# Filing stage of a graph layer: the low half of the normed x made by TensorE instead of VectorE

## The reference, cut to what matters

```python
def _layernorm(x, axis=-1, eps=1e-05):
    m = jnp.mean(x, axis=axis, keepdims=True)
    v = jnp.var(x, axis=axis, keepdims=True)
    return (x - m) / jnp.sqrt(v + eps)

edge_index_t = jnp.stack([src, dst], axis=1)
xn = _layernorm(x, axis=-1)          # x: (6250, 256), f32
x = x + gnn(xn, edge_index_t, ...) + mix(xn[None], ...)[0]
x = x + ffn(_layernorm(x, axis=-1)[None], ...)[0]
```

## Time and profile before

| | |
|---|---|
| time, median of 3 runs | 2389.4 us (2388.9 to 2390.93) |
| span of the profiled execution | 2388.4 us |
| TensorE busy (matmul) | 2128.0 us, 89% |
| VectorE busy | 1612.0 us, 67% |
| ScalarE busy | 1203.0 us, 50% |
| GpSimd busy | 358.6 us, 15% |

### The profile page before, as it was taken

How to read it: one execution, slowest core, us unless ns; L and a number is a source line. 1 busy time by engine, 2 the same in 40 slices (tenths; PEclk the granted TensorE clock), 3 DMA queues, 4 the chain that set the end, 5 groups by cost and what they waited for, 6 DMA issues and landing times.

```text
span 2388.4 us, 53411 instructions
## 1 busy us (share of the span) xinstructions
PE 2128.0 (89%) x15340; PEld 1319.0 (55%) x15341; DVE 1612.0 (67%) x4907; ACT 1203.0 (50%) x2432; POOL 358.6 (15%) x435
## 2 busy tenths in 40 slices
PE   3555557999999999999799999999999998799997
PEld 2444445555555555555355554444444443699996
DVE  6999998799999999999434342454454455455554
ACT  3445455455555555555555553444444444466664
POOL 1000000000000000000101010112112112366665
PEclk9765666899999999999899999999999999799998
DMA  3111112522222222222212114555555554555552
GB/s 81 40 34 34 39 32 71 180 111 117 111 117 110 111 120 110 119 110 117 96 51 101 51 69 177 186 207 189 189 207 188 190 206 164 166 97 91 90 92 46
DMA packets 131006, 275.62 MB, mean 115 GB/s; under 512 B 30478, under 2 KB 83903, under 8 KB 128755
## 3 DMA queue, kind: packets, MB, share of 16 engines
q1 hardware_dynamic: 103411, 221.23, 26.3%
q0 software_dynamic: 25856, 47.15, 8.8%
q10 hardware_dynamic: 1664, 6.35, 0.7%
HBM read 137.14 MB, written 132.95 MB: 113 GB/s over the span
## 4 chain that ended last, share of the span: by engine, by line
PE 80%; DVE 8%; DVEq 4%; issue 4%; DMA 1%; POOL 1%; ACT 1%; ACTq 0%; SPq 0%; POOLq 0%
PE bank L2131 45%; PE bank L2122 6%; PE bank L2352 6%; PE bank L2337 6%; PE bank L2284 5%; PE bank L2272 5%; DVE big L1043 2%; PE bank L2287 2%; DVE big L1057 1%; PE bank L2319 1%; DVEq L1072 1%; DVEq L1040 1%; DVEq L1053 1%; PE bank L2139 1%; PE bank L2000 1%
## 5 line engine op out<-in xcount | busy, mean ns | idle before, releaser
L2131 PE MATMUL bank<-RW,big 128*128 128x512 f16 (+1 forms) x4900 | 1180.9, 380 | 4.8 <-DMA big<-a_dram 4.6
L2131 PEld LDWEIGHTS bank<-RW,big 128*128 128x128 f16 x4900 | 443.9, 98 | 401.6 <-issue 9.1
L1793 ACT ACTIVATE big<-bank 128x512 f16<-128x512 f32 (+1 forms) x640 | 371.7, 581 | 318.8 <-PE bank L2122 318.8
L1190 DVE TENSOR_TENSOR big<-iotaB,keys 128x512 f16<-128x512 f16 x1300 | 452.3, 419 | 7.9 <-issue 7.8
L2122 PEld LDWEIGHTS bank<-big 128*128 128x128 f16 x2560 | 191.0, 98 | 111.7 <-issue 1.3
L2122 PE MATMUL bank<-big 128*128 128x128 f16 x2560 | 247.5, 219 | 0.4 <-issue 0.4
L908 POOL DMA_INDIRECT out_dram<-big x112 | 178.6, 1594 | 119.5 <-ACT big L1950 85.8
L844 POOL DMA_DIRECT2D big<-in_L_ffn_W_dram x8 | 6.4, 802 | 1144.1 <-DVE R L1249 1141.8
L1941 ACT ACTIVATE big<-bank,b1A,iscA 128x256 f32<-128x256 f32 x224 | 114.3, 560 | 101.1 <-PE bank L2337 97.6
L2352 PE MATMUL bank<-RW,big 128*128 (+1 forms) x1344 | 158.1, 275 | 0.0
L2337 PE MATMUL bank<-big,RW 128*128 128x256 f16 x1344 | 157.0, 274 | 0.2 <-ACT big L1930 0.2
(11 more groups left out here) (397 smaller groups left out, 2975.9 us busy)
## 6 DMA issues: line engine op xcount, KB each, us to landing
big<-a_dram SPq DMA_DIRECT2D x49, 832.0 KB, 5.9
big<-a_dram SPq DMA_DIRECT2D x49, 768.0 KB, 4.2
a_dram<-big SPq DMA_DIRECT2D x49, 640.0 KB, 3.0
a_dram<-big SPq DMA_DIRECT2D x49, 512.0 KB, 2.6
a_dram<-big SPq DMA_DIRECT2D x49, 448.0 KB, 2.5
big<-rows_dram SPq DMA_DIRECT2D x56, 265.0 KB
big<-in_x_dram SPq DMA_DIRECT2D x96, 128.0 KB, 2.1
big<-in_L_ffn_W_dram POOLq DMA_DIRECT2D x16, 512.0 KB, 4.6
```

The costliest lines, as they stand in the source:

```text
L1190: last = v.tensor_tensor(out[q].rearrange("p b (m k) -> p b m k", k=2), inturn(iotaB[:, :], QB, P // 2), twice(kd[:, q * QB:(q + 1) * QB, ...
L1793: a.activation(Ab[q][:, 0:n], banks[BB(q)][:, 0:n], ACT.Copy).then_inc(s_ab, 1)
L2131: last = mm(bank[:, :], blk(q, c), src, start=(u == 0), stop=(u == T))
```

## The change

VectorE's `low` goes, with the tile xlo and the semaphore s_xl. Instead `gram(t)` gets a group of two products in the right half of bank 5: xs with identS (f32, S on its diagonal) and then the high half in R2 with minus16 (f16, minus one on its diagonal), which together are S xs minus the high half. ScalarE evicts the low half from there. s_xt is signalled by the last of these products rather than by the last Gram product. GpSimd writes the two constants, ahead of its second signal. SyncE's blanking of R3 waits for the last s_xt.

```diff
@@ GpSimd, constants
             nc.gpsimd.memset(ident16[:, :], 0.0)
+            nc.gpsimd.memset(identS[:, :], 0.0)
+            nc.gpsimd.memset(minus16[:, :], 0.0)
...
-            for m in (ident, ident16):
-                nc.gpsimd.affine_select(out=m[:, :], in_=m[:, :], compare_op=ALU.not_equal, fill=1.0,
+            for m, one in ((ident, 1.0), (ident16, 1.0), (identS, S), (minus16, -1.0)):
+                nc.gpsimd.affine_select(out=m[:, :], in_=m[:, :], compare_op=ALU.not_equal, fill=one,
                                         base=0, pattern=[[-1, P]], channel_multiplier=1)
@@ SyncE, after the loop
-            sp.wait_ge(s_xl, T)
+            sp.wait_ge(s_xt, 1 + T)
             blank(0, at_pairs // D)
@@ VectorE
-            def low(t):
-                dve.wait_ge(s_xhi, t + 1)
-                dve.wait_ge(s_xlo, t + 1)
-                v.scalar_tensor_tensor(out=xlo, in0=xs[:, 0:D], scalar=S, in1=R2[:, bass.ds(t * 2 * D, D)],
-                                       op0=ALU.mult, op1=ALU.subtract).then_inc(s_xl, 1)
...
                 ranks(t, t % 2)
-                low(t)
@@ ScalarE
             def normal1(t):
                 act.wait_ge(s_stat, t + 1)
                 act.wait_ge(s_xt, t + 1)
-                if t:
-                    act.wait_ge(s_xl, t)
...
                 place1(t)
-                act.wait_ge(s_xl, t + 1)
-                a.activation(R2[:, bass.ds(t * 2 * D + D, D)], xlo, ACT.Copy, scale=S).then_inc(s_xlo, 1)
+                a.activation(R2[:, bass.ds(t * 2 * D + D, D)], banks[5][:, D:2 * D], ACT.Copy, scale=S).then_inc(s_xlo, 1)
@@ TensorE, gram
                 pe.wait_ge(s_xtc, t + 1)
+                pe.wait_ge(s_xlo, t + 1)
                 for h in range(2):
                     nc.tensor.transpose(banks[5][:, h * P:(h + 1) * P], xs[:, h * P:(h + 1) * P], ident[:, :])
                 for h in range(2):
-                    last = mm(banks[6 + h][:, 0:D + 1], xs[:, h * P:(h + 1) * P], xs[:, 0:D + 1],
-                              start=False, stop=False)
-                last.then_inc(s_xt, 1)
+                    mm(banks[6 + h][:, 0:D + 1], xs[:, h * P:(h + 1) * P], xs[:, 0:D + 1],
+                       start=False, stop=False)
+                mm(banks[5][:, D:2 * D], identS[:, :], xs[:, 0:D], start=True, stop=False)
+                pe.wait_ge(s_xhi, t + 1)
+                mm(banks[5][:, D:2 * D], minus16[:, :], R2[:, t * 2 * D:t * 2 * D + D], start=False, stop=True)\
+                  .then_inc(s_xt, 1)
@@ TensorE, after the loop, before bank 5 is used again
             pe.wait_ge(s_xtc, T + 1)
+            pe.wait_ge(s_xlo, T + 1)
```

More of the change, by code:

```diff
@@ L160, in gps_layer @@
         ident = sb("ident", [P, P])
+        identS = sb("identS", [P, P])
+        minus16 = sb("minus16", [P, P], F16)
         zeros16 = sb("zeros16", [P, P], F16)
@@ L264, in gps_layer @@
         xs = sp1.f32(D + 1)
-        xlo = sp1.f32(D)
         Gs = sp1.f32(2 * (D + 1)).rearrange("p (k n) -> p k n", k=2)
@@ L420, in gps_layer @@
         s_xhi = sem("s_xhi")
-        s_xl = sem("s_xl")
         s_xlo = sem("s_xlo")
```

## The result

The changed kernel takes 2373.02 us, the median of 4 runs (2371.35 to 2375.86), against 2389.39 before (4 runs as well), 16.4 us less. The two medians stand as 0.9931; the ratio estimated from all their runs is 0.9926, with an interval of 0.9912 to 0.994. Two later measurements gave 2374.66 (2373.01 to 2375.19) and 2373.76 us (2372.47 to 2373.95) for the same kernel. Each against the kernel before that ran beside it, the gain is 15.3 to 16.4 us, while VectorE's term alone, all of it kept, is 15.9.

The account below looks back on a forecast made before the run. VectorE was taken to bound the filing stage, with TensorE mostly at its slow clock. Terms -15.9 + 0.8 + 2.8 + 1.8 + 0.6 = -9.9 us took the span from 2388.4 to 2378.5, so median 2379.5; range 2375 to 2394.

Parts of the forecast that it names:

- VectorE's term: Filing stage: without `low`, 48 tiles each save 0.33 us of VectorE, 15.9 us in all.
- The constants' sum: Opening: GpSimd's two memsets and two selects delay its last select and the start by 0.8 us, all exposed.
- The tail: End of the filing stage: ScalarE waits for the last x tile, so the last two tiles can't shorten: 0.6 us.
- Charged beyond 5.88: Filing stage: losses above VectorE's new period, from restarts 2.8, falls in mid-group 1.8 and the tail 0.6 us.
- the start and six restarts: Start and after each `prepare`: TensorE begins slow, next reciprocal 0 to 0.8 us late; 7 x 0.4 = 2.8 us.
- the falls in mid-group: Filing stage: the clock falls about once in each of seven groups, mostly absorbed by slack; 7 x 0.25 = 1.8 us.
- Restless clock: Filing stage: clock falls again after some 6.6 us, 23 rounds at some 0.5 us: 2386.4 us; chance 0.23.
- TensorE becomes the bound: Filing stage: slow share stays 70%, 34 of 49 tiles take 7.2 us, 44 us lost: 2418 us; chance 0.12.
- Nearly all is kept: Filing stage: clock falls only in `prepare`, each restart hidden: -13.1 us, 2376 us; chance 0.13.
- Waiting for the deviation in place of `low`: Filing stage: VectorE waits for ScalarE instead, slow period some 6.05 us, half of 0.33 kept there; no separate chance.
- What would show it: Trace signs of being right: period 5.88, stage clock 0.8 or more, opening 0.8 us longer, fast `file1` just behind R1.
- the signs against it: Idle before reciprocals, `file1` right behind new products, `gram` over 3.6 us slow or 2.0 fast, mean clock under 0.7.

Follow-up runs that it names:

- four products more: Changed kernel with four more overwritten f32 products with identS per tile, ahead of the two that count: 2394.26 us, ratio 1.0018.
- the first experiment: Changed kernel without the two new products per tile, a copy of the transposed tile evicted as low half: 2378.18 us, ratio 0.9951.

## Why the prediction came out short

**VectorE's term was right.** The period goes from 6.21 to 5.88 us, to the hundredth.

**The constants' sum was right, and partly by luck.** 0.8 was charged as 0.3 for the memsets and 0.5 for the selects. In the nine profiles with the constants in front the first reciprocal is 0.6 to 1.0 us late, and it is back at 38.3 when they are made later. But the memsets cost nothing, and an idle of 0.4 us that nobody had foreseen stands in their place.

**The tail was about right.** It was charged for the last x tile, so it belongs to the last of the 48 periods. That one is 6.53, 7.32 and 6.27 us long in the three profiles, where 6.39 less the 0.33 would be 6.06: 0.5, 1.3 and 0.2 us lost, against 0.6. The way from the last reciprocal to the last `file1`, 0.4, 0.1 and 1.0 us longer, stood in no term.

**The failed step is "Charged beyond 5.88": the start and six restarts at 2.8 us and the falls in mid-group at 1.8.** Against the old 366.36 us less 48 x 0.33, the periods of the changed kernel lost 1.7, 2.4 and 0.3 us in its three profiles, a mean of 1.5, tail included, where these two terms and the tail had charged 5.2. Where the losses stand can be read from the waits for ScalarE's deviation: behind the start and the restarts 0.66, 0.62 and 0 us, against 2.8; behind falls in mid-group 0.19, 0.15 and 0, against 1.8. (In the last tile they are 0.25, 1.04 and 0. What is left, 0.3 to 0.6 us in each profile, is a balance of small idles of VectorE for which the profile names no wait and of tiles that had waited before.) The number of falls was about right: one in each of seven groups was expected, and the first profile has eight. What they cost was not. There are three reasons:
- The new products were priced by the ends of rows. 1.17 us slow and 0.67 fast were charged, and 1.07 and 0.54 measured (the fast f16 product is 269.47 to 269.58 in the timeline of four products more): a row's duration holds about 0.2 us in which the next instruction already runs (1.06 against 0.86). The prediction had said so for VectorE's 0.42 and 0.33 and then didn't do it for TensorE. The Trainium skill's price for a true f32 product (FP8 and Floating Point Precision, "TensorE Precision Notes": four passes), which gave an estimate of 0.85 and 0.43, was set aside for the rows; measured start to start it is 0.86 and 0.43, and the page was right.
- The loops were too long and so the slack too short. The slow loop was set at 7.2 us and is 1.62 + 1.97 + 3.26 = 6.85. The fast one was set at 4.8 and is 0.90 + 1.61 + 1.68 = 4.2. The 1.18 us taken from the earlier trace rows for a fast `file1` was not all TensorE's work. In the kernel before, `before1` waited there for VectorE's one-hot rows, as its weight load says (the rows below this list). Without `low` the one-hot rows come 0.33 us earlier, and `file1` takes 0.90 (187.76 to 188.66). So the change itself shortened TensorE's loop. The slack in a fast tile is 1.5 to 1.7 us, not 1.1, and eats what a slow tile leaves.
- The sign of the clock's part was seen, its size not. The prediction expected a mean of 0.8 or more and got 0.82, and argued that a loop bound by TensorE ends its own slow spell. It did not count that this pays. Without the products the stage loses 4.5 us to waits at a clock of 0.64, with them 1.1 at 0.82, and with ten products that feed nothing 1.2 at 0.82.

```profile
200.14 0.67 DVE L1038 TENSOR_TENSOR big<-iotaU,R 128x1000 f16<-128x1000 f16 x1
...
200.87 0.75 PEld L1990 LDWEIGHTS bank<-big 128*128 128x128 f16 x20 [0.27 <-DVE big L1038]
```

**A term was missing: the chain behind the stage.** The next stage begins only at its end, and the chain is shorter where its clock is higher: 32.2 us at 0.71 and 31.3 at 0.72 in the profiles of the kernel before and of that with the constants alone, 29.65 and 29.95 at 0.81 and 0.82, 29.0 to 29.3 at 0.85, 27.2 to 27.5 at 0.93 and 0.94. In the changed kernel's three profiles it is 2.9, 3.2 and 4.9 us shorter than in the one profile before. How much of it is due to the change is open: the first experiment has a clock of 0.64 in the stage and yet 29.1 us behind it, so the clock there isn't simply carried over, and the same kernel had it at 0.85 twice and 0.93 once.

Together: the three spans have a mean of 2373.0 us, 5.5 under the 2378.5 of the forecast. The periods are 3.7 under their terms and the chain 3.7; the way to the last `file1` (0.5), the rest (1.3) and the opening (0.1) go the other way. The 1.0 us that was added to get from the span to the median is not a fixed distance: the median here lies 1.3 us under the profiled span.

**The rivals.** *Restless clock*, at 2386.4: its time fell, but not for the reason that was given. The prediction said that the trace before shows falls only behind pauses of 1.9 and 2.04 us. It doesn't; the fall near 88.5 us comes 7 us after the rise, and the longest pause between them is 1.49; near 385.5 another fall stands behind a pause of 1.31. The rows of the first:

```profile
85.76 1.07 PE L2000 MATMUL bank<-big 128*128 128x100 f16 x20 [1.49 <-issue]
...
88.57 0.69 PE L2009 MATMUL bank<-ident,big 128*128 128x128 f32 x2 [0.93 <-ACT big L1697]
```

In the changed kernel seven of the eight falls in mid-group, 195.5 among them, come behind idles of 1.56 us or less. The Trainium skill (TensorE: Matmul & The Clock Gate, "A second HAM failure mode: psum-queue depth-cycling") says that small pauses alone can make the clock swing, and in this the trace agrees. Yet there were eight falls and not 23 rounds, and the waits behind them add up to 0.2 us at most; that the slack of the tiles around a fall takes the rest is likely, but was not tested by itself. That the clock would hold because 1.1 us is nearer to 0.93 than to 2.04 was a wrong rule that led to a nearly right count. What decides whether an idle brings a fall is not shown. *TensorE becomes the bound*, at 2418: it took four products more to get there, and then cost 18 us of periods, not 44. It had charged slow time as if the share of it were fixed. *Nearly all is kept*, at 2376, is what came out in the stage; with the chain behind it the time is lower still. *Waiting for the deviation in place of `low`*: the wait exists, and costs 0 to 1.8 us in all.

**What would show it** was borne out for the period of 5.88, the mean clock, the opening chain and for `file1` just behind R1. Of the signs against it one came in small: three reciprocals, or none in the third profile, had an idle in front that ScalarE's deviation ended. The others did not: `gram` is 3.26 us slow, under the 3.6, and outside `prepare` the periods are at VectorE's own length but for some ten, the two longest of which (9.4 and 8.53 us) were 9.73 and 8.86 before.

## What to carry to other kernels

Where an engine bounds a stage and another has room, price the moved work from start to start, not by the durations of rows, which overlap their neighbours; and ask of each leg of the receiving engine's loop what ended it: here 0.3 us of one leg was a wait for the very engine that the change relieves. If the receiving engine is TensorE at its lower clock, look at the clock as a result of the change and not as given: moved work can shorten the work around it, here by more than it cost, and the stretch behind the stage should have a line in the sum too. Test that with work that feeds nothing, which tells the clock's part from the data's.

## What the runs showed of the hardware that was not expected

- More TensorE work made TensorE less busy: 132 records more in the stage, and 11 us less busy time (201.2 to 190.3), by a mean clock of 0.82 in place of 0.65.
- Leaving out 1.07 us of slow TensorE work per tile made the kernel 3.5 to 5.2 us slower; ten f16 products of 128 columns per tile that feed nothing, run on another chip, made it 3.9 us faster again.
- The clock stayed at 1.00 for 19.2 us on end (199.8 to 219) through idles of 0.93 and 1.5 us in each 5.88 us, and had fallen near 195.5 behind idles no longer than that. The length of the last idle alone does not tell whether it falls.
- Two memsets on GpSimd cost nothing (the selects behind them start at 9.76 us against 9.75), while two selects of 128x128 cost 0.5 us and an idle of 0.4 behind them.
- ScalarE's copy of 128x256 f32 to f16 has a mean of 375 ns from PSUM (L1699), against 416 from SBUF.
